# Routing in chunks of 16 tiles, and a written-out tail of phase 1, in an attention and mixture-of-experts kernel

## What is computed

```python
x = _layernorm(x + attn(x))      # in chunks of 64 tokens: real FFT, attention on the 4 lowest
                                 # frequencies, depthwise convolution + gelu on the others,
                                 # a gate, inverse FFT
d2 = sum(xs * xs) + sum(centroid * centroid) - 2.0 * (xs @ centroid.T)
w, sel = top_k(sqrt(maximum(d2, 1e-12)), 2)
w = softmax(w)
for e in range(8):               # H = 342; we is w put at the two chosen experts
    h = silu(xs @ Wg[e] + bg[e]) * (xs @ W1[e] + b1[e])
    out = out + we[:, e:e+1] * (h @ W2[e] + b2[e])
x = _layernorm(x + out)
```

## Time and profile before

| | us |
|---|---|
| median of 3 runs | 630.18 (628.68 to 630.98) |
| profiled execution | 628.64, span 626.8 |
| phase 1 ends, last logits' copy | 237.4 |
| idx made | 283.6 |
| busy: TensorE, VectorE, ScalarE, GpSimd | 526.9, 487.8, 356.1, 302.1 |

### The profile page before, as it was taken

One profiled execution on the slowest core, in us unless ns is written; L12 is line 12 of the kernel. 1 busy time (PEld: TensorE's weight loads), 2 busy tenths in 40 slices (PEclk: granted clock), 3 DMA queues, 4 the chain that ended last, 5 costly groups with the idle time before them and its releaser, 6 DMA issues.

```text
span 626.8 us, 13674 instructions
## 1 busy us (share of the span) xinstructions
PE 526.9 (84%) x3849; PEld 494.6 (79%) x3849; DVE 487.8 (78%) x1316; ACT 356.1 (57%) x751; POOL 302.1 (48%) x480
## 2 busy tenths in 40 slices
PE   3778999999999523077999999999999999999971
PEld 2777888888897411065999999999999999999971
DVE  3668887887888256992777888889898989899983
ACT  3466788879878322023555555565647574756651
POOL 0223655654744143005444444466777676544644
PEclk9879999999999755558999999999999999999995
DMA  8142145135222210021000000011111111000000
GB/s 227 46 123 57 38 121 157 56 100 156 76 81 68 67 33 2 6 18 27 21 19 19 20 19 20 16 32 36 36 33 36 32 36 36 27 19 14 33 25 33
DMA packets 49866, 31.68 MB, mean 51 GB/s; under 512 B 14112, under 2 KB 47472, under 8 KB 49808
## 3 DMA queue, kind: packets, MB, share of 16 engines
q1 hardware_dynamic: 44864, 21.39, 12.9%
q0 software_dynamic: 4224, 8.75, 5.1%
q10 hardware_dynamic: 720, 0.82, 0.4%
HBM read 22.25 MB, written 8.69 MB: 49 GB/s over the span
## 4 chain that ended last, share of the span: by engine, by line
PE 42%; issue 9%; DVE 6%; POOL 1%; ACT 1%; DMA 1%; DVEq 0%; POOLq 0%
PE ps L1216 20%; PE ps L1234 11%; PE ps L1224 7%; PE ps L1235 4%; DVE xs L1406 3%; PE ps L1247 1%; DVE h L1389 1%; ACT hh L1310 1%; ACT xs L1276 0%; DVE mv L1346 0%; DVE maskT L929 0%; DMA xs<-rows_dram,idx 0%; DVE bn L1338 0%; POOL out_dram L1183 0%; DMA bias_parts<-blo 0%
## 5 line engine op out<-in xcount | busy, mean ns | idle before, releaser
L1216 PE MATMUL ps<-wts,xh 128*128 x624 | 154.9, 332 | 0.8 <-issue 0.7
L1234 PE MATMUL ps<-wts,hh 114*128 (+1 forms) x468 | 119.2, 340 | 4.1 <-DVE xs L1406 3.5
L1406 DVE SCALAR_TENSOR_TENSOR xs<-ps,xs 128x128 f32 x312 | 108.3, 347 | 17.6 <-DVE xs L1406 11.9
L1194 POOL TENSOR_TENSOR xl<-xT,xh 127x128 fp32r<-127x128 f32 x156 | 68.4, 458 | 106.2 <-ACT xh L1291 100.9
L1216 PEld LDWEIGHTS ps<-wts,xh 128*128 128x128 f32 x624 | 106.4, 193 | 1.3 <-issue 1.3
L1235 PE MATMUL ps<-wts,hl 114*128 (+1 forms) x468 | 104.7, 224 | 0.0
L1216 PE MATMUL ps<-wts,xl 128*128 x312 | 100.3, 321 | 0.0
L1302 ACT ACTIVATE sg<-ps 128x684 f32<-128x684 f32 x78 | 57.9, 743 | 73.8 <-PE ps L1216 73.8
L1310 ACT ACTIVATE hh<-ps 114x768 fp32r<-114x768 f32 x78 | 63.3, 812 | 57.6 <-PE ps L1224 56.0
L1234 PEld LDWEIGHTS ps<-wts,hh 114*128 114x128 f32 (+1 forms) x468 | 88.8, 190 | 7.9 <-issue 7.6
L1235 PEld LDWEIGHTS ps<-wts,hl 114*128 114x128 f32 (+1 forms) x468 | 90.3, 193 | 0.0
(11 more groups left out here) (230 smaller groups left out, 978.2 us busy)
## 6 DMA issues: line engine op xcount, KB each, us to landing
xt<-_attn_hidden_states_dram SPq DMA_DIRECT2D x8, 512.0 KB, 4.9
xres<-_attn_hidden_states_dram SPq DMA_DIRECT2D x8, 512.0 KB, 4.6
rows_dram<-x1s SPq DMA_DIRECT2D x8, 512.0 KB, 3.4
st<-in_L_ffn_W_dram SPq DMA_DIRECT2D x16, 171.0 KB
st<-in_L_ffn_Wg_dram SPq DMA_DIRECT2D x8, 171.0 KB
stl<-in_L_ffn_Wg_dram SPq DMA_DIRECT2D x8, 171.0 KB
stl<-in_L_ffn_W_dram SPq DMA_DIRECT2D x8, 171.0 KB
xs<-rows_dram,idx POOLq DMA_INDIRECT x64
```

The lines of the kernel that those rows point to most:

```text
L1194: v.tensor_tensor(xl[0:D - 1, i % 2, u, :], xT[0:D - 1, bass.ds(off[u], P)], xh[0:D - 1, i % 2, u, :].bitcast(F32), ALU.subtract).then_inc ...
L1216: mm = pe.matmul(ps[:, 2 * w + u, 0:HF], a[:, t % 2, u, :], wflat[:, bass.ds(w1[u] + (b + w * HF), HF)], start=(k == 0), stop=(k == 2))
L1234: pe.matmul(ps[:, 6 + u, 0:2 * D], hh[0:n, t % 2, u, k, :], w2flat[0:n, bass.ds(at, 2 * D)], start=(k == 0), stop=False)
L1406: v.scalar_tensor_tensor(out=row, in0=ps[:, 6 + u, k * D:(k + 1) * D], scalar=xsflat[:, bass.ds(off[2 + u], 1)], in1=row, op0=ALU.mult, op ...
```

## The change

- `steps` takes a `tail`, which each engine writes out by itself, in place of steps 8 and 9.
- TensorE in the tail: VT's transposes and the inverse transform of the last batch stand ahead of batch 6's turn. Logits take 8 columns, not 64, and batch 6's go to bank 4.
- VectorE in the tail: top_two is done for 48 tiles (three chunks of CT = 16) in two halves, the first ahead of the gate multiplies, the second behind them. The residual of the last batch is added in xt, which needs no new load. VectorE does that batch's root itself and four of its eight x1 tiles; ScalarE does the other four. GpSimd keeps three small operations.
- Still in phase 1: pair rows of three chunks (`pair_rows`), and behind the last logits' copy their sums (`pair_sums`) and ranks (`pair_ranks`), each chunk with two matmuls of 448 columns.
- Phase 2: top_two of the last 16 tiles, pair rows, two matmuls, sums and ranks of one chunk; the start of each pair (base) is added by a multiply of 1792 elements, two adds and a reduce.
- maskT is written along tiles, read from oh1 and oh2 with a stride.
- we is made by GpSimd, ahead of the bias split; VectorE's weights stop at w1 and w2.
- Constants trimb, onesb and rst are made at the start of phase 1.

The core of the diff (orders that the rows above show are left out):

```diff
+            def tail():
+                finish(B - 1, False, True)
...
+                top_two(nc, g, 0, EARLY * CT, link, False)
...
+                top_two(nc, g, 0, EARLY * CT, link, True)
+                for h in range(2):
+                    dve.wait_ge(s["z_done"], 2 * (B - 1) + h + 1)
+                    xr = xt[:, 4 * h:4 * h + 4, :].rearrange("p j d -> p (j d)")
+                    v.scalar_tensor_tensor(out=xr, in0=xr, scalar=2.0, in1=ps[:, 2 + h, :], op0=ALU.mult, op1=ALU.add).then_inc(s["zs_done"], 1)
...
+                for _ in range(3):
+                    link(v.tensor_tensor(yal[:, :], yl[:, :], yl[:, :], ALU.mult))
+                    link(v.tensor_tensor(ybl[:, :], yal[:, :], vhl[:, :], ALU.mult))
+                    link(v.scalar_tensor_tensor(out=yl[:, :], in0=ybl[:, :], scalar=1.5, in1=yl[:, :], op0=ALU.add, op1=ALU.mult))
...
+                for j in range(4):
+                    v.tensor_scalar(xres[:, j, :], xt[:, j, :], yl[:, j:j + 1], nl[:, j:j + 1], ALU.mult, ALU.add).then_inc(s["last_x1"], 1)
+                dve.wait_ge(s["r_done"], B - 1)
+                v.tensor_copy(lg[:, (B - 2) * TB:(B - 1) * TB, :], ps[:, 4, 0:TB * E].rearrange("p (j e) -> p j e", j=TB)).then_inc(s["lg_ev"], 1)
+                dve.wait_ge(s["t_done"], 2 * B - 1)
+                v.tensor_copy(x1T[:, 0:4, :].rearrange("p j m -> p (j m)"), ps[:, 7, :]).then_inc(s["last_x1t"], 1)
+                pair_rows(nc, g, 0, EARLY, link).then_inc(s["oh_early"], 1)
+                dve.wait_ge(s["r_done"], B)
+                v.tensor_copy(lg[:, (B - 1) * TB:NT, :], ps[:, 7, 0:TB * E].rearrange("p (j e) -> p j e", j=TB)).then_inc(s["lg_ev"], 1)
+                for c, (ones, trim) in enumerate(((0, 2), (1, 3), (6, 4))):
+                    dve.wait_ge(s["early_mm"], 2 * c + 2)
+                    pair_sums(nc, g, c, ones, link)
+                    pair_ranks(nc, g, c, trim, link)
...
+def pair_rows(nc, g, c0, c1, link):
+    link(v.tensor_tensor(maskT[:, :, lo:hi], oh1[:, lo:hi, :].rearrange("p t e -> p e t"), oh2[:, lo:hi, :].rearrange("p t e -> p e t"), ALU.add))
...
+def pair_sums(nc, g, c, ones, link):
+    cnt = ps[:, ones, 0:NPAIR * CT]
+    if c:
+        head = cnt.rearrange("p (a t) -> p a t", t=CT)[:, :, 0]
+        link(v.tensor_tensor(head, head, Lc[:, c - 1, :, CT - 1], ALU.add))
+    link(v.tensor_tensor_scan(Lc[:, c, :, :].rearrange("p a t -> p (a t)"), rst[:, :, :].rearrange("p a t -> p (a t)"), cnt, 0.0, ALU.mult, ALU.add))
+def pair_ranks(nc, g, c, trim, link):
+    link(v.tensor_tensor(rtmp[:, :, :], Lc[:, c, :, :], ps[:, trim, 0:NPAIR * CT].rearrange("p (a t) -> p a t", t=CT), ALU.add))
+    link(v.tensor_tensor(rtmp[:, :, :], rtmp[:, :, :], OH[:, c, :, :], ALU.mult))
+    link(v.tensor_reduce(rank[:, c * CT:(c + 1) * CT], rtmp[:, :, :].rearrange("p a t -> p t a"), AX, ALU.add))
...
+            link(v.tensor_tensor(posm[:, :, :, :], OH[:, :, :, :], base[:, :].unsqueeze(1).unsqueeze(3).broadcast_to((P, NCH, NP, CT)), ALU.mult))
+            for k in (14, 7):
+                link(v.tensor_tensor(posm[:, :, 0:k, :], posm[:, :, 0:k, :], posm[:, :, k:2 * k, :], ALU.add))
+            link(v.tensor_reduce(pos[:, :].rearrange("p (c t) -> p c t", t=CT), posm[:, :, 0:7, :].rearrange("p c a t -> p c t a"), AX, ALU.add))
+            link(v.tensor_tensor(pos[:, :], pos[:, :], rank[:, :], ALU.add))
...
+            pool.wait_ge(s_wr, 1)
+            v.tensor_tensor(we[:, :, :], oh1[:, :, :], over_e(w1[:, :]), ALU.mult).then_inc(s_wp, 1)
+            v.tensor_tensor(wo[:, :, :], oh2[:, :, :], over_e(w2[:, :]), ALU.mult).then_inc(s_wp, 1)
+            pool.wait_ge(s_wp, 2)
+            v.tensor_tensor(we[:, :, :], we[:, :, :], wo[:, :, :], ALU.add).then_inc(s_we, 1)
```

More of the change, by code:

```diff
@@ L249, in phase1, with steps @@
             preps.append((kvr[0:E if j == 7 else P, j, :], E if j == 7 else P))
-        def steps(eng, step):
+        def steps(eng, step, tail):
             step(0, True, False, False)
@@ L257, in steps @@
                 step(s_, True, True, True)
-            step(B, False, True, True)
-            step(B + 1, False, False, True)
+            tail()
         block = ctx.enter_context(nc.Block())
@@ L448, in _ @@
+            steps(pe, step, tail)
         @block.scalar
@@ L586, in _ @@
+            steps(act, step, tail)
         @block.vector
@@ L745, in _ @@
+            steps(dve, step, tail)
         @block.gpsimd
@@ L807, in phase2, with top_two @@
         experts(nc, g)
-def top_two(nc, g, lo, hi, link):
+def top_two(nc, g, lo, hi, link, second):
     v = nc.vector
@@ L814, in top_two @@
     rev = g["cr"][:, g["c2"]["rev"][0]:g["c2"]["rev"][1]]
+    m, oh = (m2, oh2) if second else (m1, oh1)
     def part(a):
@@ L844, in route @@
     NP = len(order)
-    QUARTER = NP * NT // 4
-    assert NP * NT == 4 * QUARTER and QUARTER <= 512
+    OH, Lc, rank, onesb, trimb = (g[k] for k in ("OH", "Lc", "rank", "onesb", "trimb"))
     with ExitStack() as ctx:
@@ L944, in _ @@
             dve.wait_ge(s_one, 1)
-            dve.wait_ge(s_mm, 2)
-            for c in range(4):
-                link(v.tensor_tensor_scan(csum[:, c * QUARTER:(c + 1) * QUARTER], onesf[:, :], ps[:, 4 + c, 0:QUARTER],
-                                          0.0 if c == 0 else csum[:, c * QUARTER - 1:c * QUARTER], ALU.mult, ALU.add))
-            v.memset(Sn[:, 0:1], 0.0)
-            cv = csum[0:NT, :].rearrange("p (a t) -> p a t", t=NT)
-            v.tensor_copy(Sn[:, 1:NP], cv[:, 0:NP - 1, NT - 1])
@@ new lines, in _ @@
+            link(v.tensor_copy(prT[:, :], ps[0:NP, 5, 0:NT]))
+            v.sem_inc(s_nd, 1)
+            dve.wait_ge(s_ex, 1)
+            link(v.tensor_scalar(dn[:, :], ew[:, :], 1.0, None, ALU.add))
+            link(v.reciprocal(w1[:, :], dn[:, :]))
+            v.tensor_tensor(w2[:, :], w1[:, :], ew[:, :], ALU.mult).then_inc(s_wr, 1)
+            dve.wait_ge(s_prc, 2)
+            link(v.tensor_scalar(need[:, :], ps[0:NT, 6, 0:E], 0.0, None, ALU.is_gt))
+            v.sem_inc(s_nd, 1)
+            link(v.tensor_tensor(posm[:, :, :, :], OH[:, :, :, :], base[:, :].unsqueeze(1).unsqueeze(3).broadcast_to((P, NCH, NP, CT)), ALU.mult))
```

319 lines of the change are left out of this document (232 added, 87 removed).

## The result

| | before | after |
|---|---|---|
| median, us | 630.57 (628.68 to 630.98, 4 runs) | 623.56 (622.76 to 624.06, 4 runs) |
| profiled execution, its span | 628.64, 626.8 | 623.20, 621.4 |
| last logits' copy | 237.16 | 227.30 |
| first operation of phase 2's top_two | 237.86 | 239.21 |
| ubase (L987, now L1206) | 268.60 | 262.76 |

The ratio is 0.9893 with a 95% interval of 0.987 to 0.9917: 7.0 us faster where 7.8 were forecast (622.4). In the profiled executions idx moved by 5.84 us, where the forecast had 7.75.

What follows compares the result with a forecast made beforehand. VectorE's serial chain to idx was taken as the bound, then TensorE. L987 moves from 268.60 to 256.85 + 4.0 = 260.85 us, 0.2 us of tail gain included; 630.18 - 7.8 = 622.4 us, range 616.8 to 626.8.

Steps and rivals of the forecast that it cites:

- span A: VectorE from the batch loop's end to phase 1's end: tail wins 10.7 us, chunks spend 10.1, giving 0.2 us.
- span B: VectorE from phase 1's end to L987: 11.75 us earlier without waiting, less 4.0 us of waiting for GpSimd.
- the 4.62 us from VT to the residual: Tail: present time from VT's start to VectorE's L721, kept less some 0.65 us for the removed turn of x1s.
- Narrower moving data saves perhaps a fifth: Last logits step on TensorE, 3.67 us at the lower clock: 8 columns per tile would save perhaps a fifth.
- The term read from the bounds 0.62 and 0.90 us for the reduce: Each early chunk's strided reduce of 448 elements behind the last logits, taken as 0.75 us.
- Hidden by nothing: Sums and ranks of three early chunks stand behind the last logits in VectorE's queue, adding 10.1 us.
- The waiting: Phase 2's joining chain on VectorE waits for GpSimd's we operations and blo: 4.0 us, bounds 0 to 5.7.
- It ran when GpSimd was done: L618 in the loop, 0.63 us alone, takes 1.32 us beside a GpSimd multiply; basis for the waiting costs.
- Rival 1: Joining chain in phase 2 never waits for GpSimd: 618.4 us; chance 0.23.
- Strided reading as dear as L929's write: Chunk reduces and masks read at 4.77 ns an element: +7.4 us, 629.8 us, no change; chance 0.05.
- GpSimd kept out until 271 us: VectorE's gapless chain in phase 2 delays we and biases; idx only 0.6 us earlier, 629.6 us; chance 0.04.
- A low clock in the experts: TensorE's clock stays low into the expert stage; 16 us uses up the gain, 22 us gives 633 us; chance 0.03.

Runs made afterwards that it cites:

- old order: Changed kernel with batch 6's x1s and half its turn put back ahead of VT's transposes, the second half before the inverse transform; 627.96 us, ratio 0.9956.
- rows early: Changed kernel with early chunks' pair rows ahead of the residual, two chunks' matmuls before the last turns, chunk 0's sums and ranks before the last logits' copy; 621.11 us.
- tanh: Changed kernel with bias split in the prologue, pair rows and first chunk earlier, and both softmax weights made by ScalarE from one tanh; 621.07 us, ratio 0.9851.
- biases: Changed kernel with the bias split (load, cast, subtraction, stores to DRAM) moved to the start of phase 1; 622.47 us, ratio 0.9867.
- we on VectorE: Kernel with the bias split in the prologue, and the three operations of we also moved from GpSimd to VectorE behind lob; 622.75 us, ratio 0.9884.
- biases, rows and we on VectorE: Changed kernel with bias split in the prologue, pair rows and first chunk moved forward, and we's three operations on VectorE; 620.33 us, ratio 0.9857.
- turned write: Changed kernel with the ranks' multiply writing its 448 products turned, so that the reduce reads them side by side; 625.72 us, ratio 0.9927.
- mask written turned: Changed kernel with maskT written with a stride and read along experts without one, as in the kernel before; 626.30 us, one run.

## Why the prediction was right, and where it was off

**Direction and size.** 7.0 us faster against 7.8, inside the range. idx came at 277.55 for a forecast 275.64; the 1.91 us are 1.66 in span A and 0.25 in span B. That the medians come closer than idx does is luck: the profiled execution of before, 628.64 us, lies 1.9 us below its median, that of the changed kernel, 623.20, 0.4 us below. From profile to profile it is 5.4 us, and in the second measurement 6.1.

**Where the gain comes from.** The last logits come 9.86 us earlier. The aggregates' end gives 1.90 us of this (219.19, now 217.29), the root and nl 4.43 (from there to the first x1 tile 7.16 us, now 2.73), and the tiles, turns and logits 3.53 (10.81 us, now 7.28). The runs with the old order and with the root on GpSimd test the first two; some 2.5 us of the root's part is that GpSimd's chain no longer runs beside top_two (6.36 us there, 3.85 in the run). No run undoes the last part by itself, so the 3.53 us are read from the rows and not tested. Behind the last logits the change loses: from their copy to ubase it is 35.46 us, where it was 31.44. Of these 4.02 us 3.67 are the waiting for GpSimd, and without it the routing in chunks would be no shorter than before. The forecast implies as much (226.4 to 260.85 is 34.45 us) without saying so. Chunks pay once they are worked on ahead of the last logits, as the run with rows early shows (3.98 us). No run has the new tail with the old routing, so whether that would have been faster stays open.

**Span A, to the first x1 tile: right, by two errors that cancel.** VT at 208.75 (209.15 said), the aggregates' end at 217.29 (217.0), the root at 219.99 (219.85). The forecast kept the lower level of the clock, but also the 4.62 us from VT to the residual, in which it had risen: before, the second half of the inverse transform met the rise of the clock, now nothing of it does (3.78 for 2.81 us), which makes VectorE wait a second time (0.94 us), so that from the residual's start to the aggregates' end it is 4.55 us for 3.86. The 0.69 us are hidden in part by a residual that starts 0.41 us before its forecast. The old order's run shows the size of what was missed, the second measurement how far it is a matter of when the clock's level changes.

**Span A, from there to the last logits: 0.7 us mis-sized.** The four x1 tiles take 1.11 us, not 0.7, and logits with 8 columns take 3.42 us for 16 at the lower level, where 64 columns took 3.67. "Narrower moving data saves perhaps a fifth" was an estimate without a row behind it: it saves 7%.

**Span A, the chunks: 0.8 us mis-sized.** The term read from the bounds 0.62 and 0.90 us for the reduce took 0.75, between them. It is 0.90, the upper end, which came from L964, the one row of the same kind of reading; the lower came from a row without a stride. That is three times 0.15 us; the first scan 0.83 instead of 0.65 us behind the logits' copy, and the change of block (0.54 for 0.35) make the rest. "Hidden by nothing" held: moving the sums behind the change of block made it 1.2 us worse, not better.

**Span B: 23.55 us for 23.3,** again by two errors that cancel: without waiting the chain is 19.88 us for 19.3, and the waiting 3.67 for 4.0. The waiting, a sum of 0.75, 0.85 and 1.0 for we and 1.4 for blo, was 0.79, 1.70 for the two adds together, and 1.18. It was read from one pair of rows of the loop, and two runs that took GpSimd's work away confirm it. "It ran when GpSimd was done" is right to 0.2 us only: in that pair GpSimd ends 0.90 us after L618 starts and L618 loses 0.69, and the joining multiply starts 0.94 us before L1281 ends and loses 0.79. Rival 1, no waiting, is refuted by them. The Trainium skill (SBUF — State Buffer, Who interferes with whom) says that a VectorE instruction with two SBUF inputs and GpSimd's reads of SBUF shut each other out for the whole instruction: by that rule, the runs agree (2.82 against 2.03 us, and 1.29 against 0.21 for 28 elements). Instructions with one input in SBUF kept their lengths beside GpSimd: the reduce L1197 (0.91 us) beside bhi's cast, and in the run with tanh the scan of counts from PSUM (1.09 us) beside the first multiply of we.

**The other rivals.** Strided reading as dear as L929's write: refuted, 1.80 against 4.45 ns an element. GpSimd kept out until 271 us: refuted, its operations ran at 252.86 to 261.6 us, each in a gap of VectorE's chain. A low clock in the experts: refuted, the stretch from idx to the end is 343.9 against 343.4 us (343.1 to 344.8 in all the runs, with the same code). The cover that I gave the transfers, 8 us, was there: the last copy into wts was issued by 266.8 and takes 2.4 us to land (median), idx came at 277.55.

## What to carry to other kernels

Before moving work to an idle engine, look for the place beside which it will run: GpSimd's three operations on we cost the chain that they were to relieve more than making them there would, and the profile shows the price only as longer instructions on both sides, so compare durations of the same shape. Moving work into a hole is worth as much as the hole's end moves, and where the hole let the clock fall, the work brought forward is done at half speed (the inverse transform took 3.78 us where 1.88 were measured at the upper level). When an experiment changes a short stretch of a long program, measure from a mark just ahead of it to one just behind, for what comes earlier may differ by more than the effect.

## What was not expected of the hardware

The changed kernel, run again, began its tail 1.8 us later (203.94 for 202.17), and among all profiles it is up to 3.5 us, with the same loop ahead. Two stretches of TensorE's clock sort them. The first shows in a run of 16 matmuls at 21.57 us, here before:

```profile
21.57 2.05 PE L367 MATMUL ps<-XL,qwT 128*128 128x128 f32 x16 [1.28 <-DVE XL L658]
```

and in the kernel with the root on GpSimd:

```profile
21.57 3.79 PE L388 MATMUL ps<-XL,qwT 128*128 128x128 f32 x16 [1.27 <-DVE XL L784]
```

The start is the same to 0.01 us. In the one the clock is back at its upper level by then, in the other it rises only beyond 24 us (granted 0.83 and 0.66 from 20 to 42 us). The second is at 167 to 175 us, here in the changed kernel's first profile, without a fall of the clock, and then in its second, with one:

```profile
166.15 2.00 PE L430 MATMUL ps<-kT,QB 128*128 128x64 f32 x16
```

```profile
166.21 2.94 PE L430 MATMUL ps<-kT,QB 128*128 128x64 f32 x16
```

In both TensorE was busy without a gap from 150 to 168 us. In the first the granted clock stays at 1.00, in the second it is 0.50 from 168 to 172 us, and 1.00 again from 174. The start of the tail goes by these two: with neither it is 202.1 to 202.4 us (before, the changed kernel, old order, rows early), with the late rise alone 203.8 (root on GpSimd), with the fall at 167 us alone 203.9 to 204.3 (the second profile, biases, we on VectorE, biases, rows and we on VectorE), with both 205.1 to 205.6 (sums in phase 2, turned write, mask written turned, tanh). The head goes with the second: the profiles with the fall have 17.0 us, the changed kernel's first, without it, 17.85. With the rows early no difference is left (18.93 without the fall, 18.90 and 18.92 with it). What decides over rise and fall stays open; with four to ten executions for most kernels it is a part of the spread of every ratio here, and perhaps of the 0.9 us between the two measurements of the changed kernel's gain.

Second, the lengths at which waiting engines come out are reproducible: in all eight profiles in which GpSimd has both we and the biases in phase 2 (the changed kernel twice, root on GpSimd, old order, sums in phase 2, rows early, turned write, mask written turned) the joining multiply took 2.81 or 2.82 us, the two adds 3.44 or 3.45, the small add 1.41 or 1.42. What looks like chance, two engines' instructions getting in each other's way, is fixed in these kernels: VectorE's r_w releases GpSimd's first multiply at the same place of the chain each time.
